# Graph network on one core: the row numbers of four chunks in one transfer, loaded a group ahead

## The reference

```python
s_e, v_e = s[src], v[src]                     # gather: the source node's row of each edge
w = (relu(edge_feat @ W1 + b1) @ W2 + b2)     # an 8x8 matrix per edge and path
m0, m1 = products of s_e, v_e with w and the edge's geometry
out = segment_sum(m, dst)                     # scatter: add up by target
x = layernorm(x + out)
```

## Time and profile before

| | |
|---|---|
| median of 3 runs | 4051.86 us |
| profiled execution | 4059.36 us, span 4057.4 us |
| busy PE, DVE, ACT, POOL | 3377.3, 3460.9, 2184.8, 2953.0 us |
| gathers | 1540 per layer, mean 954 and 963 ns |
| granted TensorE clock, mean | 0.908 |

### The profile page before, as it was taken

One profiled execution on the slowest core, in us unless ns is written; L12 is line 12 of the kernel. 1 busy time (PEld: TensorE's weight loads), 2 busy tenths in 40 slices (PEclk: granted clock), 3 DMA queues, 4 the chain that ended last, 5 costly groups with the idle time before them and its releaser, 6 DMA issues. The chain is left out here.

```text
span 4057.4 us, 95500 instructions
## 1 busy us (share of the span) xinstructions
PE 3377.3 (83%) x23156; PEld 1945.7 (48%) x23156; DVE 3460.9 (85%) x5277; ACT 2184.8 (54%) x6587; POOL 2953.0 (73%) x3087
## 2 busy tenths in 40 slices
PE   4777777777777777777559999999999999999996
PEld 3444444444444444444335555555555555555553
DVE  8888888888888888888759999889889888988887
ACT  3555555555555555555335565555555555555554
POOL 5777777777777777777377777777777777777772
PEclk7888888888888888888779999999999999999998
DMA  3111111111111111111212222222221222222221
GB/s 107 35 33 32 34 32 33 34 33 35 32 33 32 33 32 34 36 32 33 35 38 48 45 44 44 44 44 44 47 45 41 47 44 44 44 43 44 44 44 28
DMA packets 238827, 162.68 MB, mean 40 GB/s; under 512 B 143937, under 2 KB 212594, under 8 KB 238066
## 3 DMA queue, kind: packets, MB, share of 16 engines
q1 hardware_dynamic: 104338, 91.78, 8.7%
q0 software_dynamic: 98560, 50.66, 8.6%
q10 hardware_dynamic: 35650, 17.88, 1.7%
HBM read 148.83 MB, written 10.43 MB: 39 GB/s over the span
## 5 line engine op out<-in xcount | busy, mean ns | idle before, releaser
L430 POOL DMA_INDIRECT rows<-x_rows,src x1540 | 1483.2, 963 | 536.6 <-issue 526.6
L430 POOL DMA_INDIRECT rows<-in_x,src x1540 | 1468.9, 954 | 485.6 <-issue 472.3
L775 PE MATMUL red<-prod,ident 128*128 128x336 f32 (+1 forms) x4704 | 1511.2, 475 | 1.4 <-DVE prod L1073 1.2
L775 PEld LDWEIGHTS red<-prod,ident 128*128 128x128 f32 x4704 | 892.3, 195 | 635.4 <-issue 193.3
L1073 DVE TENSOR_TENSOR prod<-wps,arena 128x896 f32<-128x896 f32 x782 | 832.4, 1083 | 176.2 <-PE wps L762 159.0
L755 PE MATMUL wps<-bias_parts,ones 64*128 64x448 bf16 (+1 forms) x2346 | 471.4, 398 | 610.7 <-DVE prod L1067 452.4
L565 ACT ACTIVATE gap<-iota,slot_plan 128x128 bf16<-128x128 f32 x3136 | 935.6, 386 | 7.0
L762 PE MATMUL wps<-w_sb,hidden 64*128 64x448 f32 (+1 forms) x3920 | 746.9, 476 | 0.0
L583 ACT ACTIVATE arena<-red 128x336 f32<-128x336 f32 (+1 forms) x294 | 135.5, 461 | 1103.5 <-PE red L775 1102.9
L755 PEld LDWEIGHTS wps<-bias_parts,ones 64*128 64x128 bf16 x2346 | 114.6, 94 | 1135.3 <-DVE prod L1067 562.4
L1082 DVE TENSOR_REDUCE arena<-prod 128x384 f32<-128x3072 f32 (+1 forms) x195 | 520.9, 2671 | 0.1
(11 more groups left out here) (127 smaller groups left out, 3025.3 us busy)
## 6 DMA issues: line engine op xcount, KB each, us to landing
mlp<-in_dist SPq DMA_DIRECT2D x196, 256.0 KB
fetched<-in_x SPq DMA_DIRECT2D x3072, 0.1 KB
fetched<-x_rows SPq DMA_DIRECT2D x3072, 0.1 KB
mlp<-in_feat SPq DMA_DIRECT2D x98, 256.0 KB
rows<-in_x,src POOLq DMA_INDIRECT x1540
rows<-x_rows,src POOLq DMA_INDIRECT x1540
frames<-frame ACTq DMA_DIRECT2D x49, 144.0 KB
geo<-frames ACTq DMA_DIRECT2D x98, 72.0 KB
```

The lines of the kernel that those rows point to most:

```text
L430: nc.gpsimd.indirect_dma_start(out=rows[z][:, t, :], out_offset=None, in_=table_rows, in_offset=bass.IndirectOffsetOnAxis(ap=src_sb[z][:, ...
L775: ins = nc.tensor.matmul(red[:, bank * 512:bank * 512 + cols], ident[:], pr[:, i, :, a:b, :], start=(i == 0), stop=(i == MUL - 1))
```

## The change

The row numbers of a whole group (four chunks, 32 KB) come in one transfer. There are two buffers of 64 columns, and group h + 1 is loaded while group h is gathered: SP issues it in the fourth chunk's step of group h, behind that chunk's `mlp` load. The first group's load stands ahead of the loop. POOL waits for `src_loaded` once a group, and its loop and SP's hold two groups, since buffers alternate; they turn 12 times per layer.

```diff
-        src_sb = slots(lambda z: sb(f"src{z}", [P, TILES], I32))
+        src_sb = slots(lambda b: sb(f"src{b}", [P, FETCH_CHUNKS * TILES], I32))
...
+        def src_loads(eng, j, pair, b):
+            return eng.snap(j * (FETCH_PAIRS + 1 - b) + (pair + 1))
...
-            def load_source(n, z, r, k):
-                s = layers[n]
-                sp.wait_ge(s.rows_read[z], r)
-                sp.dma_start(src_sb[z][:], src[bass.ds(k, 1)].rearrange("k p t -> p (k t)")
-                             ).then_inc(s.src_loaded[z], 16)
+            def load_source(n, b, group):
+                sp.dma_start(src_sb[b][:], src[bass.ds(group, 1)].rearrange("g p t -> p (g t)")
+                             ).then_inc(layers[n].src_loaded[b], 16)
...
-                            load_source(n, z, r, k)
                             load_mlp(n, z, r, k)
+                            if m == FETCH_CHUNKS - 1:
+                                sp.wait_ge(s.rows_read[RING - 1], r0)
+                                load_source(n, 1 - b, h + 1)
...
+                    for z in range(RING):
+                        sp.wait_ge(s.rows_read[z], round_of(sp, j, 0))
+                    load_source(n, 0, 0)
+                    with sp.Fori(0, FETCH_PAIRS) as pair:
+                        group(pair * 2, 0)
+                        group(pair * 2 + 1, 1)
...
                 pool.wait_ge(s.rows_read[z], r)
                 pool.wait_ge(s.rows_copied[z], r)
-                pool.wait_ge(s.src_loaded[z], r * 16 + 16)
+                if m == 0:
+                    pool.wait_ge(s.src_loaded[b], loads * 16)
...
-                        in_offset=bass.IndirectOffsetOnAxis(ap=src_sb[z][:, t:t + 1], axis=0),
+                        in_offset=bass.IndirectOffsetOnAxis(ap=src_sb[b][:, m * TILES + t:m * TILES + t + 1], axis=0),
...
-                    with pool.Fori(0, FETCHES) as h:
-                        for m in range(FETCH_CHUNKS):
-                            gather(n, m % RING, round_of(pool, j, h * FETCH_ROUNDS + m // RING),
-                                   TILES - (1 if m == FETCH_CHUNKS - 1 else 0))
+                    with pool.Fori(0, FETCH_PAIRS) as pair:
+                        for b in range(2):
+                            for m in range(FETCH_CHUNKS):
+                                i = pair * (2 * FETCH_ROUNDS) + (b * FETCH_ROUNDS + m // RING)
+                                gather(n, m % RING, round_of(pool, j, i), m, b, src_loads(pool, j, pair, b),
+                                       TILES - (1 if m == FETCH_CHUNKS - 1 else 0))
```

More of the change, by code:

```diff
@@ L38 @@
 FETCHES = ROUNDS // FETCH_ROUNDS
+FETCH_PAIRS = FETCHES // 2
+SRC_GROUPS = FETCHES + 1
 LN_EPS = 1e-5
@@ L228, in ring @@
                     return made
-                self.src_loaded = ring("src_loaded", 16)
+                self.src_loaded = slots(lambda b: sem(f"l{n}_src_loaded{b}"))
                 self.geo_loaded = ring("geo_loaded", 16)
@@ L362, in stream, with group @@
                 with sp.Fori(0, count) as j:
-                    with sp.Fori(0, FETCHES) as h:
+                    def group(h, b):
                         f = sp.snap(j * FETCHES + h + 1 + n * (count * FETCHES))
@@ L389, in stream @@
                         r = round_of(sp, j, ROUNDS - 1)
-                        load_source(n, z, r, (ROUNDS - 1) * RING + z)
                         load_mlp(n, z, r, (ROUNDS - 1) * RING + z)
@@ L419, in _, with gather @@
                                            bass.bass_isa.ReduceOp.max).then_inc(spans_known, 1)
-            def gather(n, z, r, tiles=TILES):
+            def gather(n, z, r, m, b, loads, tiles=TILES):
                 s = layers[n]
@@ L448, in gather_all @@
                 with pool.Fori(0, count) as j:
-                    with pool.Fori(0, FETCHES) as h:
-                        for m in range(FETCH_CHUNKS):
-                            gather(n, m % RING, round_of(pool, j, h * FETCH_ROUNDS + m // RING),
-                                   TILES - (1 if m == FETCH_CHUNKS - 1 else 0))
+                    with pool.Fori(0, FETCH_PAIRS) as pair:
[4 more added lines that the diff above has]
+                                       TILES - (1 if m == FETCH_CHUNKS - 1 else 0))
                     for z in range(RING):
-                        gather(n, z, round_of(pool, j, ROUNDS - 1), LAST_TILES if z == RING - 1 else TILES)
+                        gather(n, z, round_of(pool, j, ROUNDS - 1), z, 0, src_loads(pool, j, FETCH_PAIRS, 0),
+                               LAST_TILES if z == RING - 1 else TILES)
                     reset_counts(n, round_of(pool, j, ROUNDS - 1))
@@ L1428 @@
         "x_self": x_pad.reshape(SELF_CHUNKS, 4, P, FEAT).transpose(1, 3, 0, 2).reshape(P, SELF_CHUNKS, P),
-        "src": by_partition(padded(src, EDGES, 0)),
+        "src": padded(src, SRC_GROUPS * FETCH_CHUNKS * CHUNK, 0).reshape(SRC_GROUPS, FETCH_CHUNKS * TILES, P).swapaxes(1, 2),
         "src_fetched": padded(src, EDGES, 0).reshape(CHUNKS, TILES, P)[FETCH_CHUNKS - 1:FETCHES * FETCH_CHUNKS:FETCH_CHUNKS,
```

## The result

| | before | after |
|---|---|---|
| median, 18 runs each | 4052.22 us | 4059.51 us |
| lowest to highest | 4048.19 to 4053.63 | 4054.14 to 4064.79 |
| ratio, 95% interval | | 1.0019 [1.0012, 1.0027] |
| profiled execution | 4059.36 | 4062.61 |
| first to last gather, layer 0 | 1945.2 | 1957.8 |

The changed kernel is slower by 7.3 us. It has a gain in layer 1 and a larger loss in layer 0. The two profiled executions stand only 3.2 us apart, since the one of before lies 7.1 us above its median and the one of after 3.1 us above its own.

The account below looks back on a forecast made before the run. POOL's gathers, one every 1.25 us, were taken to bound the kernel; 1.8 + 1.3 + 0.9 = 4.0 us regained early in layer 1 took the median from 4051.9 to 4047.9 us, own range 4043 to 4052, wider range 4038 to 4060.

Parts of the forecast that it names:

- the second group's stall: POOL's idle before layer 1's second group: 1.8 us come back, not 4.1, since DVE's reduction then holds the start.
- the third group's: POOL's wait for src before layer 1's third group: all of the stall goes, 1.3 us.
- the gap behind it: Idle of 1.81 us before the third gather of layer 1's third group: 0.9 us goes, as part of the same stall.
- The even groups' gap: POOL idles 0.8 to 0.9 us before every second group's third gather, 12 times in layer 0; taken as staying.
- INC kept its alternation: INC_SWDGE_SEM on POOL takes 1.1 us in one group and 2.1 in the next; expected to go on so.
- rivals 2 and 3: 2: even groups' gap goes with loop's turn, 4036 us (0.10); 3: POOL's longer loop pays at its turn, 4080 (0.07).
- the first gathers: The layers' first gathers on POOL were to start still at 26.3 and 2027 us: 0 gain.
- The 4 us are kept: After layer 1's early groups DVE, at 19.5 us a chunk, falls no further behind POOL, so the gain stays.
- SP's time is hidden as long as its mlp loads and fetched rows are in time ... 0.: SP loses 146 of 196 issues with their waits and half its loop turns; claimed worth 0, as loads hang on DVE and PE.
- I take it as staying: 0; ends -12 and +14: Gap at every second group's third gather: 0 change; -12 us if it goes, +14 if it comes in every group.
- 2 us either way: Layer 1's longer gathers, 1.0 to 1.4 us for 0.95, come and go with DVE's phase: 2 us faster or slower.
- The fourth: Rival: the 0.6 us gap in each group, or POOL's registers uncovered, 14 to 19 us slower, about 4064 (0.06).

Follow-up runs that it names:

- three unchanged kernels named above: Kernel before with POOL's loop of two groups, with 34816 bytes of descriptor scratch, or with INC_SWDGE_SEM ahead of the fourth chunk's gathers: 4050.78, 4051.19, 4050.45 us.
- a_paced_all: Changed kernel with SP's wait for rows_read put back ahead of every mlp load, the last round's two included: 4046.00 us, ratio to before 0.9989.
- experiment 3: Changed kernel with layer 0's mlp load cut to 64 of 512 columns (32 KB for 256 KB), SP unpaced: 4048.95 us, ratio to before 0.9996.

## Why the prediction was wrong

**What held.** The three terms of the sum: the second group's stall 1.8 (1.7 measured), the third group's 1.3 (1.3), the gap behind it 0.9 (1.0), with the new releaser named. The three unchanged kernels named above have 4.33 to 5.15, 1.55 to 1.86 and 1.81 at these places, so the gain is no accident of one profile. The even groups' gap kept its count and place; INC kept its alternation; POOL's longer loop cost nothing and left the gap where it was, in a run of its own (rivals 2 and 3 fall); the first gathers came at 26.3 and no later in layer 0, though at 2039.8 in layer 1, which is layer 0's loss handed on. "The 4 us are kept" is true of layer 1. Where the loss is taken away, the kernel is 5.0 us faster than before (a_paced_all), close to the 4.0 worked out, and that version's median, 4046.00, lies in the forecast's own range.

**The step that failed** is the one on SP: "SP's time is hidden as long as its mlp loads and fetched rows are in time ... 0." It asked only whether SP's work could be late. Without its wait SP's work came early. The wait for `rows_read` belonged to the load of row numbers, but it paced the whole queue behind it, and so the 256 KB of each `mlp` load. Freed, the load went at the moment at which POOL's third gather hangs on rows in flight. The price in layer 0, between the two profiled executions: 6.1 us in the gaps and 6.7 in longer gathers, with 0.2 us less elsewhere, 12.6 in all; in layer 1 about 1.6 us in the last gap. Against the three kernels of before's time the longer gathers are 9 to 11 us and the whole of layer 0 is 15 to 17. Layer 1 gives back 3 to 5 of it; kernel by kernel the two layers together lose 10 to 13 us. The profiled execution of after lies 3.1 us above its median, which leaves 7 to 9 us for the 7.3 us of the medians.

**Two further steps rested on the same blind spot.** "I take it as staying: 0; ends -12 and +14" bounded the gap by its count alone. I had read its size at three places and not asked what it waits for; a gap whose sizes are that even looked like a constant of POOL's. And the longer gathers were put down to DVE's phase, "2 us either way", for layer 1 only. In layer 0 they cost 6.7 us against the one profile of before and 9 to 11 against the three others, and follow the transfer (experiment 3).

**The rivals.** None was right. The fourth came nearest in price, 14 to 19 us by "little things"; the places it named, a gap in every group and uncovered registers, do not show. The sign was to be had from the change itself: in the first three chunks of a group SP's row that waits for `rows_read` is gone, and the row behind it issues a large transfer.

## What to carry over

A wait that is removed from an in-order queue was also a pace for everything behind it: ask of each instruction behind it not only whether it could be late, but when it will now be issued, and which wait of the bounding engine is open at that moment. An engine whose gathers are queued far ahead can still have a place where it seems to hang on a transfer just issued; look for idle time put to "issue" that comes at a fixed place, and don't put a large load there. If a wait goes for its stall's sake, keep the pace elsewhere: here one `wait_ge` ahead of each large load, those of the last round included, turned a loss of 7.3 us into a gain of 5.0; without the last round's it was 1.6, which the interval doesn't tell from none. And before a difference between two profiles is put down to the change, see how far apart the profiles of kernels of equal time lie.

## What was not expected of the hardware

- Once in 126 gathers (two groups) POOL's third gather of a group starts no earlier than 2.22 us after the landing of the last gather of the group ahead, at 240 of 240 places. `dynamic_dma_scratch_size`, the length of POOL's loop, and the place and number of INC_SWDGE_SEM don't move the place; behind a stall of the queue the gap is 1.36 to 1.82 us though the landing is long past.
- With a 256 KB transfer of SP's issued 0.5 us behind it, a gather's first packet came 2.50 us after its issue for 1.65, and its rows landed 2.8 us after it for 2.1. With 32 KB in as many packets, 2.2 us.
- The same transfers made POOL's gathers longer as its trace shows them: 1475.65 us over 1540 gathers, for 1466.85 with 32 KB loads and 1464.5 to 1466.7 in three kernels whose loads go elsewhere. Why the issuing side feels them stays open.
